# A graph kernel's prologue: order of the small groups' power, three fused weight products moved behind the first convolutions, fusion softmax between them

## The chip, the cores and the metric

One core of one Trainium2 chip. The metric is device time of one execution in microseconds; lower is better. The engines are PE (TensorE: matrix products and transpositions), DVE (VectorE), ACT (ScalarE), POOL (GpSimd) and SP (SyncE, which here only issues transfers).

## What is computed

Inputs are x (64 graphs of 128 nodes with 128 features) and adj (64 matrices of 128 x 128). Two blocks follow one another, each added to its input and layer-normalised:

```
x = layernorm(x + groups(x, adj))        # 5 groups of the first 25 nodes, two convolutions each
x = layernorm(x + gnn(x, adj != 0))      # 5 layers of message passing with a GRU cell
groups: A = adj_g + I; norm = dinv * A * dinv, dinv = (row sum of A) ** -0.5
        h = relu(norm @ (x_g @ W1[g]) + b1[g]); out_g = relu(norm @ (h @ W2[g]) + b2[g])
        sum over g of softmax(fusion_w)[g] * out_g, added into the nodes of the group
gnn, layer l: m = h @ weight[l]; agg = A.T @ m; gi = agg @ w_ih.T + b_ih; gh = h @ w_hh.T + b_hh
        r, z = sigmoid(i + h parts); n = tanh(i_n + r * h_n); h = (1 - z) * n + z * h
```

The kernel multiplies each layer's weight into the input weights beforehand (weight[l] @ w_ih.T, 128 x 384): these five products are the fused weights. For precision every operand of the large products is kept as a rounded high part and the remainder, its low part; a product is three matmuls.

## The kernel before, in words

The batch is cut into 4 chunks of 16 graphs, a chunk into 4 visits of 4 graphs. The message passing runs in 80 windows (5 layers x 4 visits x 4 chunks): window k makes the 18 gate products of one layer of one visit on PE, with the gates on ACT, DVE and POOL; the group convolutions of the next chunk are laid between the products of the current one by window number (the class Plan: adjacency, neighbours Y, hidden HA and HB, second SA and SB, outputs). Those of chunk 0 have no windows to lie between and make up the prologue, with the preparation of the weights. The order of work on each engine is written out by hand, one program per engine, and semaphores join them; an engine runs its program strictly in that order.

The prologue up to the first window (lines of the kernel before):

- Transfers. SP issues the small groups' adjacency rows, x rows (xt) and W2, then waits for ac_zero = 2, which POOL gives when it has cleared the later chunks' buffer (L450), and goes on with chunk 1's rows and the full x and adj of chunk 0. ACT issues w_ih, weight, w_hh, W1 and the bias rows (L586 to L590, between the high weights). POOL issues some adjacency and x rows, later eight adjacency rows of chunk 1 and the node mask (L452, L453).
- Degrees and power. DVE sums the rows (degrees, L705), POOL raises the sums to the power -1/2 in two instructions (power, L370: the large group's 4 tiles TA first, the small groups' 5 tiles TB second). DVE scales (scaled_part, L738) and expands the large group into block diagonals (spread, L748); POOL expands the small groups (spread, L376).
- PE runs 20 dummy transpositions (stay_warm, L1128), turns the weights (L1143 to L1151), makes fused weights 0 to 3 (L998) into the PSUM banks 3, 4, 6, 7, then 6 dummies, the transpositions of the block diagonals (first_adjacency, L1017, with 8 more dummies after the first), the products with x (neighbours, L1054), the transposition of the bias rows (L1162), the hidden and second products (L1063, L1073, L1080), the outputs (L1110, L1118), the mask's transposition (L1175), fused weights 4, 8 dummies, and the transposition of the gathered sums (back_visit, L1137) as soon as DVE has gathered them.
- High and low weights. ACT rounds each fused product into wf (high_weights, L504), DVE subtracts that from the PSUM bank for the low part (low_weights, L838). ACT makes the high parts of layers 0 to 3 ahead of the adjacency, 4 behind the outputs. DVE makes the low parts one by one between its other work.
- Fusion softmax. DVE subtracts the maximum (L903), POOL takes the exponential (L455), DVE divides (L909 to L914, signal b_ok); ACT's outputs (L543, L552) need it. DVE does this behind its copies second_b1 and second_b2.
- Then DVE gathers (L795), adds to x (L802), takes statistics (L828, L832); POOL makes deviations (L429 to L434) behind the ones of one adjacency visit (L407); ACT, DVE and POOL normalise; PE turns the result (L1187) and the windows begin.

Semaphores that matter: pow_ok (power), prep_f (a fused product is in its bank), prep_hi and prep_lo (its high, low part is made), b_ok, s_ps and o_ps (second products, outputs), mask_in, gathered.

Of the kernel before, what the change touches and what calls it, by code (L numbers as in the profile page):

```python
# [14 lines left out]
GATES = 3 * D  # L15
# [78 lines left out]
def made(k):  # L94

    return SLOTS + 1 if k == SLOTS - 1 else SLOTS if k == SLOTS else k + 1
# [33 lines left out]
def build(nc, x, adj, nodemask, W1, b1, W2, b2, fusion_w, weight, w_ih, w_hh, b_ih, b_hh, out):  # L130
# [3 lines left out]
    with ctx:  # L134
# [66 lines left out]
        wlt = cg[:].rearrange("p o (l d) -> p (o l) d", d=D)[:, 0:LAYERS, :]  # L201
        wit = ng[:, 0, 0:GATES]

        st1, ag1 = sb("st1", [128, SLOTS, SB, 6]), sb("ag1", [128, SLOTS, SB, 2])
# [7 lines left out]

        WF_BANKS = (3, 4, 6, 7, 3)

# [9 lines left out]
        def b1c(g, c):  # L224
# [9 lines left out]
        ac_pool_in = [sem(f"ac{c}_pool_in") for c in range(2)]  # L234
        wit_ok, wlt_ok, table_ok, sub_ok, f0_ps, x0_ok, a0_ok = map(sem, (
            "wit_ok", "wlt_ok", "table_ok", "sub_ok", "f0_ps", "x0_ok", "a0_ok"))
        ident_ok, ac_zero, dve_c, pool_c, exp_ok = map(sem, ("ident_ok", "ac_zero", "dve_c", "pool_c", "exp_ok"))
# [120 lines left out]
        def _(pool):  # L358
# [11 lines left out]
            def power(c):  # L370

                pool.wait_ge(deg_ok, c + 1)
                for some in (slice(0, len(TA)), slice(len(TA), NT)) if c == 0 else (slice(0, NT),):
                    nc.gpsimd.tensor_tensor(dinv[:, c, some], safe[:, some], minus_half[:, some], ALU.pow).then_inc(pow_ok, 1)
# [114 lines left out]
        def _(act):  # L489
# [11 lines left out]
            def high_weights(l):  # L501

                act.wait_ge(prep_f, l + 1)
                nc.scalar.copy(wf[:, l, 0, :], P[WF_BANKS[l]][:, 0:GATES]).then_inc(prep_hi, 1)  # L504

            def adjacency(c):
# [27 lines left out]
            def second_a(c):  # L534

                act.wait_ge(s_ps, 3 * c + 1)
                nc.scalar.copy(s2[0:ROWS[0], 0:4, :],
                               banks(c)["s"][0][0:ROWS[0], :].rearrange("p (t d) -> p t d", t=4)).then_inc(sa_ok, 1)
# [8 lines left out]
            def output_b(c):  # L547

                act.wait_ge(o_ps, 2 * c + 2)
                for g in range(1, NG):  # L550
                    a, b = group_cols(g)
                    nc.scalar.activation(part[:, a:b], banks(c)["o"][1][:, a:b], ACT.Relu, bias=fb2[:, g:g + 1],  # L552
                                         scale=fw[:, g:g + 1]).then_inc(ob_ok, 1)
# [36 lines left out]
            load_rows(NG * HC + NG + 3, b_hh.rearrange("(c h) -> c h", h=128))  # L590
            high_weights(2)
            high_weights(3)
            adjacency(0)
# [10 lines left out]
            output_a(0)  # L604
            output_b(0)
            high_weights(4)
            nc.scalar.copy(maskc[:], P[3][:, GATES:GATES + B]).then_inc(prep_a, 1)
# [80 lines left out]
        def _(dve):  # L688
# [49 lines left out]
            def scaled_part(tiles):  # L738

                part_ = slice(tiles[0], tiles[-1] + 1)  # L740
                dve.wait_ge(pow_ok, 1 if tiles is TA else 2)
                dve.wait_ge(prep_c, 4)
                link(TT(dinv[:, 0, part_], dinv[:, 0, part_], zero[:, part_], ALU.mult))
                if tiles is TB:
                    TT(am[:, part_, :], am[:, part_, :], dinv[:, 0, part_].unsqueeze(2).to_broadcast(am[:, part_, :].shape),
                       ALU.mult).then_inc(am_ok, 1)
# [88 lines left out]
            def low_weights(l):  # L835

                dve.wait_ge(prep_hi, l + 1 if l < 4 else l + 2)
                TT(wf[:, l, 1, :], P[WF_BANKS[l]][:, 0:GATES], wf[:, l, 0, :], ALU.subtract).then_inc(prep_lo, 1)  # L838

# [47 lines left out]

            degrees(0)
            low_weights(0)
            scaled_part(TA)  # L890
            spread(0)
            spread(1)
            scaled_part(TB)
            spread(2)
            spread(3)
            low_weights(1)
            adjacency(0)
            neighbours(0)
            dve.wait_ge(prep_hi, 5)
            TT(wh[:, 1, :], P[1][:, 0:GATES], wh[:, 0, :], ALU.subtract).then_inc(prep_lo, 1)  # L900
# [3 lines left out]
            hidden_b0(0)  # L904
            low_weights(2)
            second_b1(0)
            second_b2(0)
            dve.wait_ge(exp_ok, 1)
# [5 lines left out]
            TT(fb2[:], biasc[:, NG * HC:BI], fw[:], ALU.mult).then_inc(b_ok, 1)  # L914
            low_weights(3)
            gather(0)
# [9 lines left out]
            dve.wait_ge(prep_a, 2)  # L926
            low_weights(4)
            lo_neighbours(0, PG)
# [5 lines left out]
            for w in ALL_WINDOWS:  # L934
# [46 lines left out]
                if w.sg + 2 < CHUNKS and w.i == Plan.SCALED:  # L981
                    scaled(w.sg + 2)
            final = B // SB - 1
            norm2(final - 3)
# [8 lines left out]
        def _(pe):  # L993
# [23 lines left out]
            def first_adjacency():  # L1017

                pe.wait_ge(bda_ok, 1)
                turn_adjacency(0, 0)  # L1020
                stay_warm(8, P[5])
                pe.wait_ge(bdb_ok, 1)
                turn_adjacency(0, 4)
                turn_adjacency(0, 5)
                pe.wait_ge(bda_ok, 2)
                turn_adjacency(0, 1)
                pe.wait_ge(bdb_ok, 2)
                turn_adjacency(0, 6)
                pe.wait_ge(bda_ok, 3)
                turn_adjacency(0, 2)  # L1030
                pe.wait_ge(bdb_ok, 3)
                turn_adjacency(0, 7)
                pe.wait_ge(bda_ok, 4)
                turn_adjacency(0, 3).then_inc(t_ps, 1)
                pe.wait_ge(bdb_ok, 4)
                turn_adjacency(0, 8).then_inc(t_ps, 1)
# [117 lines left out]
            pe.wait_ge(wlt_ok, 1)  # L1154
            for l in range(4):
                fused_weights(l)
            stay_warm(6, P[5])
            first_adjacency()
# [15 lines left out]
            pe.wait_ge(mask_in, 16)  # L1174
            TR(P[3][:, GATES:GATES + B], maskr[:], ident[0:B, 0:B])  # L1175
            fused_weights(4)
            stay_warm(8, P[4])
            pe.wait_ge(gathered, ADDS)
            for visit in range(SLOTS):
                back_visit(visit)  # L1180
            stay_warm(18, PR)
            for _ in range(12):
                MM(PR[:, 0:128], wh[:, 0, 0:128], wh[:, 0, 128:256], start=True, stop=True)

# [22 lines left out]
            def enter(visit, bank):  # L1207
# [6 lines left out]
                turn(bank, entering(visit)).then_inc(X_ps, 1)  # L1214

            enter(0, PL)
            pe.wait_ge(a0_ok, 1)
            aggregate(0, PG, entering(0))

            for w in ALL_WINDOWS:  # L1220
                k, s = w.k, w.slot
                xhi, xlo = hhi[:, s, :], hlo[:, s, :]
                pe.wait_ge(hi_ok, made(k))
                if k == 0:

                    pe.wait_ge(x0_ok, SLOTS)
                    gates = ((PR, 0), (PH, 2), (PZ, 1))
# [62 lines left out]
                if k == 0:  # L1290
                    pe.wait_ge(a0_ok, 2)
                    pe.wait_ge(prep_lo, 6)
                    aggregate(1, PT, entering(1))
# [43 lines left out]
```

## Time and profile before

| | |
|---|---|
| time, median of 3 runs | 546.04 us (545.37 to 546.91) |
| profiled execution, span from first to last instruction | 544.4 us; the page gives it no time of its own |
| PE busy | 519.5 us, 95% of the span |
| DVE / ACT / POOL busy | 437.8 / 368.6 / 250.2 us |
| mean granted TensorE clock | 0.983 of full |

The span is the time from the first to the last instruction; a run's time also holds what lies around it. Shares are averages over the prologue (about 36 us before PE turns the first normalised visit), the windows and a short end.

### The profile page before, as it was taken

Reading aid. Unit: us, or ns where it says so; the run is one execution under the profiler, and the core shown is the slowest. Engines: PE = TensorE matmul, PEld = TensorE weight load, DVE = VectorE, ACT = ScalarE, POOL = GpSimd, SP = SyncE. Lnnn points to the kernel's source line nnn. Section 1 sums busy time; section 2 is a strip of 40 time slices with the busy share of each in tenths; the row PEclk is TensorE's granted clock in tenths of the full one; section 3 lists DMA queues with packets and bytes.
Section 4 is the critical chain, followed back from the end, with each engine's and each line's share of the span. In section 5 each row is a group of like instructions: output and inputs, shape, how many; then the busy total and the mean of one; then the engine's idle time right before and its main releaser. Section 6 shows DMA issues by size and latency. Waiting matters only on the chain.

```text
span 544.4 us, 8517 instructions
## 1 busy us (share of the span) xinstructions
PE 519.5 (95%) x2991; PEld 443.9 (82%) x2991; DVE 437.8 (80%) x965; ACT 368.6 (68%) x681; POOL 250.2 (46%) x301
## 2 busy tenths in 40 slices
PE   7998899999999999999999999999999999999970
PEld 5886788888888889888888888888888888888850
DVE  4488566689989986789988986778988998878785
ACT  2446566577786676787776676687795678777644
POOL 6659222258642254448652245446542244423235
PEclk8999899999999999999999999999999999999995
DMA  5867610000000010000000000000000000100002
GB/s 141 198 178 183 161 32 5 1 0 1 2 0 1 1 32 20 21 20 21 0 2 1 0 1 21 20 20 20 0 2 1 1 1 20 39 20 0 1 0 78
DMA packets 35564, 17.29 MB, mean 32 GB/s; under 512 B 4306, under 2 KB 35483, under 8 KB 35523
## 3 DMA queue, kind: packets, MB, share of 16 engines
q1 hardware_dynamic: 32489, 15.12, 10.5%
q10 hardware_dynamic: 2393, 1.41, 0.9%
q8 instruction: 24, 0.39, 0.3%
q0 software_dynamic: 640, 0.22, 0.3%
q14 instruction: 18, 0.14, 0.1%
HBM read 12.54 MB, written 4.19 MB: 31 GB/s over the span
## 4 chain that ended last, share of the span: by engine, by line
PE 88%; DVE 6%; ACT 2%; DMA 1%; issue 1%; ACTq 1%; POOL 1%; DVEq 0%; POOLq 0%
PE p L1200 19%; PE p L1202 19%; PE p L1201 19%; PE p L1194 13%; PE p L1187 8%; PE p L1080 3%; PE p L1054 2%; PE p L1073 1%; PE p L1063 1%; DVE hT L866 1%; PE p L998 1%; DMA zg<-in_L_gnn_weight_dram 1%; DVE cg L965 1%; PE p L1004 1%; DVE cg L968 1%
## 5 line engine op out<-in xcount | busy, mean ns | idle before, releaser
L470 POOL TENSOR_TENSOR dg<-hT,ng 128x512 f32<-128x512 f32 x80 | 125.9, 1574 | 266.2 <-ACT ng L672 266.2
L1200 PE MATMUL p<-ghi,wf 128*128 128x512 f32 x240 | 101.2, 422 | 2.0 <-DVE glo L858 1.9
L1200 PE MATMUL p<-hhi,wh 128*128 128x512 f32 x237 | 100.1, 422 | 0.0
L1202 PE MATMUL p<-ghi,wf 128*128 128x512 f32 x240 | 94.5, 394 | 0.0
L1201 PE MATMUL p<-glo,wf 128*128 128x512 f32 x240 | 93.6, 390 | 0.0
L1202 PE MATMUL p<-hhi,wh 128*128 128x512 f32 x237 | 93.3, 394 | 0.0
L1201 PE MATMUL p<-hlo,wh 128*128 128x512 f32 x237 | 92.6, 391 | 0.0
L965 DVE SCALAR_TENSOR_TENSOR cg<-p,biasc,rg 128x512 f32<-128x512 f32 x80 | 59.8, 748 | 39.0 <-ACT rg L656 38.0
L656 ACT ACTIVATE rg<-p,gb 128x512 f32<-128x512 f32 x80 | 55.4, 692 | 36.6 <-PE p L1202 30.9
L672 ACT ACTIVATE ng<-cg,biasc 128x512 f32<-128x512 f32 x80 | 57.9, 724 | 23.1 <-DVE cg L968 22.9
L1194 PEld LDWEIGHTS p<-an,nat 128*128 128x128 f32 x512 | 67.2, 192 | 7.4 <-DVE glo L858 2.2
L1194 PE MATMUL p<-an,nat 128*128 128x128 f32 x512 | 67.9, 276 | 2.0 <-DVE glo L858 2.0
L852 DVE TENSOR_TENSOR hlo<-hT,hhi 128x512 fp32r<-128x512 f32 x76 | 66.7, 878 | 1.0
L670 ACT ACTIVATE zg<-p,gb 128x512 f32<-128x512 f32 x80 | 55.0, 688 | 17.8 <-PE p L1202 17.8
L968 DVE TENSOR_TENSOR cg<-cg,p 128x512 f32<-128x512 f32 x80 | 55.0, 687 | 8.7 <-DVE cg L965 0.5
L858 DVE TENSOR_TENSOR glo<-p,ghi 128x512 fp32r<-128x512 f32 x80 | 55.2, 690 | 7.3 <-ACT ghi L623 7.2
L866 DVE TENSOR_TENSOR hT<-ng,dg 128x512 f32<-128x512 f32 x80 | 56.9, 712 | 2.8
L1187 PE MATMUL p<-ident,hT 128*128 128x128 f32 x320 | 49.0, 276 | 7.4 <-DVE hT L866 7.3
L864 DVE TENSOR_TENSOR dg<-zg,dg 128x512 f32<-128x512 f32 x80 | 55.2, 690 | 0.0
L1187 PEld LDWEIGHTS p<-ident,hT 128*128 128x128 f32 x320 | 38.6, 142 | 18.8 <-DVE hT L866 12.0
L1202 PEld LDWEIGHTS p<-ghi,wf 128*128 128x128 f32 x240 | 45.0, 188 | 10.5
L652 ACT COPY nat<-p 128x512 f32<-128x512 f32 x64 | 37.6, 588 | 22.7 <-PE p L1187 21.8
(147 smaller groups left out, 855.2 us busy)
## 6 DMA issues: line engine op xcount, KB each, us to landing
xn<-in_x_dram SPq DMA_DIRECT2D x8, 512.0 KB, 4.8
an<-in_adj_dram SPq DMA_DIRECT2D x8, 512.0 KB, 7.2
out_dram<-xn SPq DMA_DIRECT2D x16, 256.0 KB, 2.3
xt<-in_x_dram SPq DMA_DIRECT2D x16, 50.0 KB
w<-in_L_gnn_W_dram ACTq DMA_DIRECT2D x1, 640.0 KB, 6.1
w<-in_L_gnn_W_dram SPq DMA_DIRECT2D x1, 640.0 KB, 6.3
zg<-in_L_gnn_weight_dram ACTq DMA_DIRECT2D x1, 320.0 KB, 4.0
xt<-in_x_dram SPq DMA_DIRECT2D x8, 36.0 KB
```

The source lines that it names most:

```text
L470: nc.gpsimd.tensor_tensor(dg[:, w.k % 2, :], hT[:, w.slot, :], ng[:, w.k % 2, :], ALU.subtract).then_inc(d_ok, 1)
L656: nc.scalar.activation(rg[:, p, :], PR[:], ACT.Sigmoid, bias=gb[:, 0:1]).then_inc(r_ok, 1)
L672: nc.scalar.activation(ng[:, p, :], cg[:, p, :], ACT.Tanh, bias=bin_).then_inc(n_ok, 1)
L852: TT(hlo[:, m % SLOTS, :], hT[:, m % SLOTS, :] if source is None else source[:], hhi[:, m % SLOTS, :], ALU.subtract).then_inc(lo_ok, 1)
L866: TT(hT[:, s, :], ng[:, p, :], dg[:, p, :], ALU.add).then_inc(h_ok, 1)
L965: STT(cg[:, p, :], PH[:], bhn, rg[:, p, :], ALU.add, ALU.mult).then_inc(t1_ok, 1)
L968: TT(cg[:, p, :], cg[:, p, :], PI[:], ALU.add).then_inc(c_ok, 1)
L1187: last = TR(bank[:, q * 128:(q + 1) * 128], src(q), ident[:])
L1194: last = MM(bank[:, q * N:(q + 1) * N], src(q), an[:, b + q, :], start=True, stop=True)
L1200: MM(bank[:], w[:, 0, cols], xhi, start=start, stop=False)
L1201: MM(bank[:], w[:, 0, cols], xlo, start=False, stop=False)
L1202: return MM(bank[:], w[:, 1, cols], xhi, start=False, stop=stop)
```

## The change

- POOL raises the small groups to the power first; DVE scales them first and then scales and expands the large group. The low weights of layers 0 and 1 come behind these.
- PE makes only fused weights 0 and 1 ahead of the adjacency; 2, 3 and 4 come behind the outputs, layer 3 into bank 0 instead of 7. The dummies after the fused weights (6), inside first_adjacency (8) and behind fused weights 4 (8) are left out; the later dummies write another bank.
- ACT copies fused products 2 to 4 also into SBUF (kept, a view of s2, which is free then); DVE subtracts from there, in windows 3, 4 and 5. PE waits for kept_ok ahead of the first turn and the first window, and for the low parts at the first window of layers 2 to 4; ACT's next write of s2 waits for the last subtraction.
- DVE does the softmax ahead of second_b1 and second_b2.

```diff
@@ -200,6 +200,7 @@
         wl = zg[:].rearrange("p o (l d) -> p (o l) d", d=D)[:, 0:LAYERS, :]
         wlt = cg[:].rearrange("p o (l d) -> p (o l) d", d=D)[:, 0:LAYERS, :]
         wit = ng[:, 0, 0:GATES]
+        kept = s2[:].rearrange("p (l q) d -> p l (q d)", l=3)
 
         st1, ag1 = sb("st1", [128, SLOTS, SB, 6]), sb("ag1", [128, SLOTS, SB, 2])
         rs1, nm1 = sb("rs1", [128, SLOTS, SB]), sb("nm1", [128, SLOTS, SB])
@@ -210,7 +211,7 @@
         PR, PH, PZ, PI, PT, PG, PL, PM = P
 
 
-        WF_BANKS = (3, 4, 6, 7, 3)
+        WF_BANKS = (3, 4, 6, 0, 3)
 
         ALONE = dict(adj=(P[0], P[2]), y=(P[5], P[4]), ha=(P[0], P[2]), hb=(P[5], P[3]), s=(P[4], P[1], P[0]),
                      o=(P[2], P[5]))
@@ -232,8 +233,8 @@
         ac_in = [sem(f"ac{c}_in") for c in range(CHUNKS)]
         ac_act_in = sem("ac_act_in")
         ac_pool_in = [sem(f"ac{c}_pool_in") for c in range(2)]
-        wit_ok, wlt_ok, table_ok, sub_ok, f0_ps, x0_ok, a0_ok = map(sem, (
-            "wit_ok", "wlt_ok", "table_ok", "sub_ok", "f0_ps", "x0_ok", "a0_ok"))
+        wit_ok, wlt_ok, table_ok, sub_ok, f0_ps, x0_ok, a0_ok, kept_ok = map(sem, (
+            "wit_ok", "wlt_ok", "table_ok", "sub_ok", "f0_ps", "x0_ok", "a0_ok", "kept_ok"))
         ident_ok, ac_zero, dve_c, pool_c, exp_ok = map(sem, ("ident_ok", "ac_zero", "dve_c", "pool_c", "exp_ok"))
         prep_t, prep_a, prep_f, prep_hi, prep_lo, fw_ok, b_ok = map(sem, (
             "prep_t", "prep_a", "prep_f", "prep_hi", "prep_lo", "fw_ok", "b_ok"))
@@ -370,7 +371,7 @@
             def power(c):
 
                 pool.wait_ge(deg_ok, c + 1)
-                for some in (slice(0, len(TA)), slice(len(TA), NT)) if c == 0 else (slice(0, NT),):
+                for some in (slice(len(TA), NT), slice(0, len(TA))) if c == 0 else (slice(0, NT),):
                     nc.gpsimd.tensor_tensor(dinv[:, c, some], safe[:, some], minus_half[:, some], ALU.pow).then_inc(pow_ok, 1)
 
             def spread(c):
@@ -502,6 +503,8 @@
 
                 act.wait_ge(prep_f, l + 1)
                 nc.scalar.copy(wf[:, l, 0, :], P[WF_BANKS[l]][:, 0:GATES]).then_inc(prep_hi, 1)
+                if l >= 2:
+                    nc.scalar.copy(kept[:, l - 2, :], P[WF_BANKS[l]][:, 0:GATES]).then_inc(kept_ok, 1)
 
             def adjacency(c):
 
@@ -534,6 +537,8 @@
             def second_a(c):
 
                 act.wait_ge(s_ps, 3 * c + 1)
+                if c == 1:
+                    act.wait_ge(prep_lo, 6)
                 nc.scalar.copy(s2[0:ROWS[0], 0:4, :],
                                banks(c)["s"][0][0:ROWS[0], :].rearrange("p (t d) -> p t d", t=4)).then_inc(sa_ok, 1)
 
@@ -588,8 +593,6 @@
             high_weights(1)
             load_rows(NG * HC + NG, b_ih.rearrange("(c h) -> c h", h=128))
             load_rows(NG * HC + NG + 3, b_hh.rearrange("(c h) -> c h", h=128))
-            high_weights(2)
-            high_weights(3)
             adjacency(0)
             neighbours(0)
             act.wait_ge(prep_t, 4)
@@ -603,6 +606,8 @@
             act.wait_ge(b_ok, 1)
             output_a(0)
             output_b(0)
+            high_weights(2)
+            high_weights(3)
             high_weights(4)
             nc.scalar.copy(maskc[:], P[3][:, GATES:GATES + B]).then_inc(prep_a, 1)
 
@@ -738,7 +743,7 @@
             def scaled_part(tiles):
 
                 part_ = slice(tiles[0], tiles[-1] + 1)
-                dve.wait_ge(pow_ok, 1 if tiles is TA else 2)
+                dve.wait_ge(pow_ok, 1 if tiles is TB else 2)
                 dve.wait_ge(prep_c, 4)
                 link(TT(dinv[:, 0, part_], dinv[:, 0, part_], zero[:, part_], ALU.mult))
                 if tiles is TB:
@@ -834,8 +839,14 @@
 
             def low_weights(l):
 
-                dve.wait_ge(prep_hi, l + 1 if l < 4 else l + 2)
-                TT(wf[:, l, 1, :], P[WF_BANKS[l]][:, 0:GATES], wf[:, l, 0, :], ALU.subtract).then_inc(prep_lo, 1)
+                if l < 2:
+                    dve.wait_ge(prep_hi, l + 1)
+                    product = P[WF_BANKS[l]][:, 0:GATES]
+                else:
+                    dve.wait_ge(prep_hi, l + 2)
+                    dve.wait_ge(kept_ok, l - 1)
+                    product = kept[:, l - 2, :]
+                TT(wf[:, l, 1, :], product, wf[:, l, 0, :], ALU.subtract).then_inc(prep_lo, 1)
 
             def half_norm1(visit, some):
 
@@ -886,25 +897,20 @@
                 last.then_inc(ln2_st, 1)
 
             degrees(0)
+            scaled_part(TB)
+            scaled_part(TA)
+            for t in TA:
+                spread(t)
             low_weights(0)
-            scaled_part(TA)
-            spread(0)
-            spread(1)
-            scaled_part(TB)
-            spread(2)
-            spread(3)
             low_weights(1)
             adjacency(0)
             neighbours(0)
-            dve.wait_ge(prep_hi, 5)
+            dve.wait_ge(prep_hi, 3)
             TT(wh[:, 1, :], P[1][:, 0:GATES], wh[:, 0, :], ALU.subtract).then_inc(prep_lo, 1)
             dve.wait_ge(fw_in, 16)
             link(nc.vector.tensor_reduce(fmx[:], fw[:], AX.X, ALU.max, negate=True))
             TS(fw[:], fw[:], fmx[:], None, ALU.add).then_inc(sub_ok, 1)
             hidden_b0(0)
-            low_weights(2)
-            second_b1(0)
-            second_b2(0)
             dve.wait_ge(exp_ok, 1)
             link(nc.vector.reduce_sum(fsum[:], fw[:], AX.X))
             link(nc.vector.reciprocal(fsum[:], fsum[:]))
@@ -912,7 +918,8 @@
             dve.wait_ge(prep_a, 1)
             TT(gb[:], biasc[:, BI:BI + 2], biasc[:, BI + 3:BI + 5], ALU.add)
             TT(fb2[:], biasc[:, NG * HC:BI], fw[:], ALU.mult).then_inc(b_ok, 1)
-            low_weights(3)
+            second_b1(0)
+            second_b2(0)
             gather(0)
             ones(0)
             add_visit(0)
@@ -924,7 +931,6 @@
             add_visit(3)
             lo_state(0, PL)
             dve.wait_ge(prep_a, 2)
-            low_weights(4)
             lo_neighbours(0, PG)
             norm1(2)
             ones(1)
@@ -980,6 +986,8 @@
                     lo_neighbours(k + 2, PG)
                 if w.sg + 2 < CHUNKS and w.i == Plan.SCALED:
                     scaled(w.sg + 2)
+                if k in (3, 4, 5):
+                    low_weights(k - 1)
             final = B // SB - 1
             norm2(final - 3)
             leave(final - 1, PT)
@@ -1018,7 +1026,6 @@
 
                 pe.wait_ge(bda_ok, 1)
                 turn_adjacency(0, 0)
-                stay_warm(8, P[5])
                 pe.wait_ge(bdb_ok, 1)
                 turn_adjacency(0, 4)
                 turn_adjacency(0, 5)
@@ -1152,9 +1159,8 @@
             last.then_inc(prep_t, 1)
             pe.wait_ge(wit_ok, 1)
             pe.wait_ge(wlt_ok, 1)
-            for l in range(4):
-                fused_weights(l)
-            stay_warm(6, P[5])
+            fused_weights(0)
+            fused_weights(1)
             first_adjacency()
             neighbours(0)
             nr = NG * HC + NG + 6
@@ -1173,14 +1179,15 @@
             output_b(0)
             pe.wait_ge(mask_in, 16)
             TR(P[3][:, GATES:GATES + B], maskr[:], ident[0:B, 0:B])
+            fused_weights(2)
+            fused_weights(3)
             fused_weights(4)
-            stay_warm(8, P[4])
             pe.wait_ge(gathered, ADDS)
             for visit in range(SLOTS):
                 back_visit(visit)
-            stay_warm(18, PR)
+            stay_warm(18, PG)
             for _ in range(12):
-                MM(PR[:, 0:128], wh[:, 0, 0:128], wh[:, 0, 128:256], start=True, stop=True)
+                MM(PG[:, 0:128], wh[:, 0, 0:128], wh[:, 0, 128:256], start=True, stop=True)
 
             def turn(bank, src):
                 for q in range(SB):
@@ -1213,6 +1220,7 @@
                     pe.wait_ge(ln1_dve, 1)
                 turn(bank, entering(visit)).then_inc(X_ps, 1)
 
+            pe.wait_ge(kept_ok, 1)
             enter(0, PL)
             pe.wait_ge(a0_ok, 1)
             aggregate(0, PG, entering(0))
@@ -1221,8 +1229,11 @@
                 k, s = w.k, w.slot
                 xhi, xlo = hhi[:, s, :], hlo[:, s, :]
                 pe.wait_ge(hi_ok, made(k))
+                if w.i % SLOTS == 0 and 2 <= w.l and w.sg == 0:
+                    pe.wait_ge(prep_lo, w.l + 2)
                 if k == 0:
 
+                    pe.wait_ge(kept_ok, 3)
                     pe.wait_ge(x0_ok, SLOTS)
                     gates = ((PR, 0), (PH, 2), (PZ, 1))
                     for bank, g in gates:
@@ -1289,7 +1300,6 @@
                 product(PZ, wl_now, 1, xhi, xlo, False, True).then_inc(z_ps, 1)
                 if k == 0:
                     pe.wait_ge(a0_ok, 2)
-                    pe.wait_ge(prep_lo, 6)
                     aggregate(1, PT, entering(1))
                 if k in (1, 2):
                     pe.wait_ge(glo_ok, 2 * k - 1)
```

## Rows read from the trace of the kernel before

**Rows 1.** The profile page: span, chain by engine, and one group of its costliest (columns named there).
```profile
span 544.4 us, 8517 instructions
...
PE 88%; DVE 6%; ACT 2%; DMA 1%; issue 1%; ACTq 1%; POOL 1%; DVEq 0%; POOLq 0%
...
L852 DVE TENSOR_TENSOR hlo<-hT,hhi 128x512 fp32r<-128x512 f32 x76 | 66.7, 878 | 1.0
```

**Rows 2.** Chain of waits, 8 to 60 us: start, us, what.
```profile
9.73 4.51 PE p L998 x8
14.24 0.66 PE p L1131 x6
...
15.86 0.59 PE p L1004 x7
...
16.97 2.22 PE p L1054 x18
```

**Rows 3.** Stretches: PE, PEld, DVE, ACT, POOL busy (x); PEclk, DMA share, GB/s.
```profile
5.00:10.00 5.00, 3.40 (x18) 2.65 (x18) 1.43 (x5) 2.62 (x5) 3.23 (x8) 1.00 0.65 163
10.00:15.00 5.00, 5.00 (x17) 2.94 (x16) 2.83 (x9) 1.92 (x4) 3.66 (x8) 0.66 0.89 260
...
55.00:60.00 5.00, 3.56 (x21) 2.77 (x19) 4.30 (x8) 4.36 (x8) 0.53 (x1) 1.00 0.22 58
60.00:70.00 10.00, 9.36 (x55) 8.60 (x56) 3.68 (x9) 3.73 (x9) 3.00 (x2) 0.83 0.77 192
```

**Rows 4.** PE in order of time: start, us, instruction.
```profile
28.82 0.91 PE L998 MATMUL p<-ng,cg 128*128 128x384 f32 x2
```

**Rows 5.** POOL in order of time; idle before and its releaser in brackets.
```profile
9.82 2.19 POOL L374 TENSOR_TENSOR dinv<-safe,minus_half 128x4 f32<-128x4 f32 x2 [1.48 <-DVE safe L727]
13.36 1.56 POOL L395 TENSOR_TENSOR bdb<-am,ksel 72x144 f32<-72x144 f32 x5 [1.34 <-DVE am L745]
...
16.27 4.73 POOL L263 DMA_DIRECT2D ac<-in_adj_dram  x8 [0.29 <-POOL fused L451]
...
21.52 1.26 POOL L455 TENSOR_TENSOR fw<-euler,fw 128x5 f32<-128x5 f32 x1
29.74 2.02 POOL L407 TENSOR_SCALAR an<-an 128x512 f32<-128x512 f32 x1 [6.96 <-DMA an<-in_adj_dram]
33.79 0.20 POOL L429 TENSOR_SCALAR rs<-ag 128x4 f32<-128x4 f32 x1 [2.02 <-DVE ag L832]
```

**Rows 6.** VectorE in order of time, prologue.
```profile
13.19 0.90 DVE L751 SCALAR_TENSOR_TENSOR bda<-am,dinv,ksel 100x100 f32<-100x100 f32 x2
...
16.56 1.18 DVE L760 TENSOR_SCALAR nb<-p,dinv 72x72 f32<-72x72 f32 x5 [2.00 <-PE p L1004]
...
25.35 0.42 DVE L779 COPY s<-p 72x256 f32<-72x256 f32 x1 [2.02 <-PE p L1080]
...
27.20 0.14 DVE L909 TENSOR_REDUCE fsum<-fw 128x1 f32<-128x5 f32 x1
...
28.00 0.55 DVE L838 TENSOR_TENSOR wf<-p,wf 128x384 fp32r<-128x384 f32 x1
```

**Rows 7.** Stretches of half a microsecond, PE alone: busy (x), PEclk, DMA share, GB/s.
```profile
14.50:15.00 0.50, 0.50 (x7) 1.00 1.18 314
...
16.50:17.00 0.50, 0.06 (x2) 1.00 0.07 22
```

**Rows 8.** DMA issues, 0 to 50 us: KB, median us from issue to landing.
```profile
maskr<-in_nodemask_dram POOLq DMA_DIRECT2D x1, 32.0 KB, 6.7
```

**Rows 9.** ScalarE in order of time, prologue.
```profile
30.07 0.49 ACT L504 CAST wf<-p 128x384 fp32r<-128x384 f32 x1
...
35.58 0.88 ACT L562 ACTIVATE xn<-xn,nm,rs 128x128 f32<-128x128 f32 x2 [4.91 <-POOL nm L434]
```

**Rows 10.** VectorE in order of time, behind windows 3 and 4.
```profile
76.93 0.75 DVE L965 SCALAR_TENSOR_TENSOR cg<-p,biasc,rg 128x512 f32<-128x512 f32 x1 [2.25 <-ACT rg L656]
...
81.46 1.06 DVE L773 TENSOR_SCALAR hb<-p,biasc 128x144 f32<-128x144 f32 x4 [1.03 <-PE p L1073]
```

## The prediction

> **What bounds the kernel now.** I read the page first, then the chain of waits, then the engines in order of time over the first 45 us, because everything the change moves lies there or has its price there. The chain that ended last runs through PE for 88% of the span [rows 1]: from about 61 us to the end PE is hardly ever without work, so nothing done on the other engines in the 80 windows shows unless PE waits for it, and a microsecond taken out of the prologue is a microsecond taken from the end. The prologue's own chain [rows 2] is PE as well: eight records of fused weights (four layers) from 9.73 to 14.24, then dummy transpositions (14 of them, with one real one among them) to 15.86, 0.59 us of real ones, and from 16.97 the convolutions. The clock explains why the fused weights are so long: between 10 and 15 us the mean granted clock was 0.66, which is 3.4 us at 0.5 (1.2 GHz) and the rest at 1 (2.4 GHz), after five microseconds in which PE had work for 3.40 [rows 3]; the one layer made later took 0.91 us with its tail [rows 4], not 4.51 / 4 = 1.13.
>
> **What the change does, step by step** (times are those of the profiled execution).
>
> **1. Power and expansion.** The two powers take 2.19 us on POOL from 9.82, and POOL then idles 1.34 us, since the small groups, which POOL itself expands, come second [rows 5]. With the small groups first their power is ready at about 10.95 (half of 2.19), VectorE scales them while POOL makes the second power, and POOL's five expansions (1.56 us) start at about 12.05 instead of 13.36: done at 13.6, not 14.9. VectorE's four expansions can start at about 12.25; the pair beside POOL's work took 0.90 [rows 6], so four take at most 1.8, to 14.0. The two low-weight subtractions now come behind them, 0.55 each [rows 6], to 15.1.
>
> **2. PE to the end of the adjacency.** Two of four layers go (half of 4.51, 2.25 us) and with them the dummies from 14.24 to 15.86, 1.62 us: 3.9 us less work ahead of the 0.59 us of transpositions. Not all of it is gained: PE is free at 12.0 but the last expansion comes at about 14.0, so the adjacency ends at about 14.3 instead of 16.45, 2.15 earlier.
>
> **3. Neighbours.** These are 18 records, 2.22 us [rows 2]. The large group's 8 follow at once (14.8 to 15.8). The small groups need VectorE's five scalings, 1.18 us [rows 6], which now start at 15.1, behind the second subtraction, and end at 16.3. PE's 10 records trail them: about 16.9, instead of 19.18, 2.3 earlier.
>
> **4. A wait that comes up behind it.** PE next transposes the bias rows, before directly behind the neighbours at 19.19 [rows 2]; their four loads and those of the small groups' x were issued by 13.0, and no view shows when they landed. Bounds: not before the queues drained, not after 19.19. The DMA share was 1.18 at 14.5 to 15.0 and 0.07 at 16.5 to 17.0 [rows 7], so I take 17.2, nearest to the second row, and the step becomes 1.95 instead of 2.3. Were they as early as 15, the gain stays 2.3; as late as 19, there is none.
>
> **5. The convolutions** shift as one piece, if the clock holds, since PE works there without a gap. The softmax is moved into a place where VectorE waited 2.02 us for PE (before 25.35) and takes 0.80 (27.20 to 28.00) [rows 6]. Its exponential is POOL's, 1.26 us, behind eight adjacency loads that POOL issues from 16.27 on and the mask's [rows 5]; all of that moves up by 1.3, so it ends at 21.5, the softmax at 22.4, and the copy behind it is wanted at 25.35 - 1.95 = 23.4. Cover left: 1.0 us. If POOL is later than that, second_b1 and all PE work behind it wait.
>
> **6. Fused weights 2 to 4 after the outputs.** Before, one layer and eight dummies lay in PE from 28.82 until the gathered sums came at 30.98, 2.16 us [rows 2, 4]. Three layers take 2.0 to 2.25 (0.65 to 0.75 each: the second record overlaps the first one's tail) and at most 3 x 0.91 = 2.7: zero to 0.55 us late; I take zero. The mask that PE waits for ahead of them took 6.7 us to land [rows 8] from its issue right behind those loads, at 16.27 + 4.73 = 21.0, so it was there at 27.7 and was read before 28.82; issued 1.3 earlier it is there at 26.4, wanted at about 26.7. ScalarE's six copies and the mask's (7 x 0.49 at most, 3.4 us, of which 1.0 was there before) go into its wait of 4.91 us before 35.58 [rows 9]: nothing, with 2.5 left.
>
> **7. POOL ahead of the layer norm.** It waits for the adjacency until 29.74, makes ones of it for 2.02, to 31.76, and is wanted at 33.79 [rows 5], after the change at 31.84. The load is released by POOL's memset, 1.3 us earlier; even unmoved it would just do. Nothing.
>
> **8. Low weights in windows 3, 4 and 5.** VectorE then waits for others for 2.25, 1.03 and, the third time, longer than that [rows 10]; two of the three waits stand there. A subtraction costs between 0.55 and, by the mean of a wider one whose inputs both lie in SBUF, 0.88 [rows 6, 1]: covered. The Trainium skill (SBUF — State Buffer, "Who interferes with whom") says that a DVE instruction with two SBUF inputs contends with a GpSimd instruction that reads SBUF, which would speak for the upper end, as that mean does; the sum is zero by either. The removed subtraction between the first state and neighbours stood in a wait for ScalarE: nothing.
>
> **Sum:** 2.15 by step 2, 2.3 by step 3, cut to 1.95 by step 4; nothing from 5 to 8. The span goes from 544.4 [rows 1] to 542.45. The page gives no time of its own for this execution; the median of the runs, 546.04, is 1.6 above its span, and I carry that over: **544.1 us**. About 0.3% (1.6 us) is what a measurement of this kernel can tell from no change, so the forecast lies only just on the faster side.
>
> **The rivals.**
> **A. The clock takes the gain.** The 22 dummies kept PE busy; without them it waits between 12.0 and 14.8 for most of the time. Before, five microseconds with work for 3.56 were followed by ten with a mean clock of 0.83, again 3.4 us at 0.5 [rows 3]. If such a stretch falls on the neighbours and first hidden products, it loses 1.7 of 1.95: 545.8. For it: PE's work from 12.7 to 14.3 is sparse. Against: the stretch between 10 and 15 ended while PE was fed without a break, and the neighbours and the convolutions are dense. The Trainium skill (TensorE: Matmul & The Clock Gate, "What's actually happening") puts it as a rule: the throttled state is the default and activity releases it; that speaks against taking the dummies out, and the rows agree that idle time precedes the fall.
> **B. Slower.** The same mechanism, lasting: half clock from about 14.8 until well into the second convolution, two such stretches. The convolutions are bound by PE, so 6.8 us at 0.5 cost 3.4, more than the 1.95: 547.5. It turns to the slower side once PE runs 3.9 us of this work at half clock. Against: rows 3 show two such stretches, 50 us apart, and none that lasts.
> **C. More gain.** The loads are there at 16.9 (2.3 gained, 543.7), or the half clock after 60 us [rows 3] does not come when the same work arrives 2 us earlier; it costs up to 1.7, so 544.1 - 1.7 = 542.4.
> **D. The wait only moves.** The bias rows land near 19, or POOL's longer way to the exponential holds the softmax: PE waits where it worked before, 546.0.
>
> **The numbers.** Forecast 0.52, A 0.16, B 0.08, C 0.16, D 0.08. About three quarters of the forecast's own spread (half a microsecond each way, from steps 4 and 6) lies past 0.3%: 0.39, with C 0.55 for faster. The rest of it, A and D make 0.37 within 0.3%, B 0.08 slower. The range runs from C's lower value to a little past D: 542.3 to 546.3, and leaves out B and the tail of C.
>
> **What would show it.** Right: the first expansions on POOL at about 12.1; PE's adjacency ending near 14.3; a short PE idle before the bias rows, which start near 17.2; the gathered sums transposed near 29.0; ScalarE's wait before the first norm shrunk to under 2 us; first window's products 1.9 us earlier, and window 20 as well. Wrong: half clock after 14 us (A, B), a PE wait before the bias rows beyond 18 or a VectorE wait for the exponential (D), a second copy in VectorE held up in windows 3 to 5, or a late mask in front of the fused weights.

## The result, and the profile after

| | before | changed |
|---|---|---|
| median | 545.35 us (10 executions, 543.45 to 546.95) | 548.04 us (10 executions, 546.27 to 549.13) |
| ratio to before, 95% interval | 1 | 1.0045 [1.0026, 1.0064] |
| span of the profiled execution | 544.4 us | 546.7 us |

The changed kernel is 0.45% slower by the ratio (the medians lie 2.7 us apart), where 1.95 us less was forecast. In the experiments further down, one execution of the filled kernel (754 us) and one of the reordered kernel (2974 us) were disturbed and are left out of the ratios; the second was the profiled one, so no trace of that kernel is read. (Line numbers in the rows of the changed kernel and of the experiments are those of each kernel; the operands name the step. L1006 is now a fused product, L1061 the neighbours, L1070 and L1080 the hidden products, L1087 the second ones.)

The chain of waits of the changed kernel, to be held against [rows 2]:

```profile
10.63 5.81 DMA xt<-in_x_dram
16.44 0.04 issue
16.49 2.45 PE p L1061 x10
18.93 0.22 PE p L1168
19.16 2.96 PE p L1070 x4
...
30.54 2.13 PE p L1006 x6
32.67 0.45 PE p L1144 x4
```

PE in order of time in the same execution (the bracket is PE's idle time before the row and what ended it):

```profile
12.95 0.29 PE L1012 MATMUL p<-ident,bda 100*100 100x100 f32 x1 [1.87 <-DVE bda L756]
...
14.66 1.11 PE L1061 MATMUL p<-na,xt 100*128 100x100 f32 x8 [0.44 <-ACT na L515]
16.49 2.45 PE L1061 MATMUL p<-nb,xt 72*128 72x72 f32 x10 [0.72 <-DMA xt<-in_x_dram]
...
19.09 3.03 PE L1070 MATMUL p<-ya,w 128*128 128x400 f32 x4
21.91 2.41 PE L1080 MATMUL p<-yb,w 128*128 128x144 f32 x16
...
32.51 1.69 PE L1144 MATMUL p<-ident,fused 128*25 128x128 f32 x14
```

The same records of small groups, hidden products and back transposition in the kernel before:

```profile
17.91 1.28 PE L1054 MATMUL p<-nb,xt 72*128 72x72 f32 x10
...
19.28 1.61 PE L1063 MATMUL p<-ya,w 128*128 128x400 f32 x4
20.73 1.96 PE L1073 MATMUL p<-yb,w 128*128 128x144 f32 x16
...
30.98 1.93 PE L1137 MATMUL p<-ident,fused 128*25 128x128 f32 x16 [0.37 <-DVE fused L795]
```

And stretches of the changed kernel, with the columns of [rows 3]:

```profile
10.00:15.00 5.00, 2.69 (x16) 1.49 (x15) 3.50 (x11) 1.79 (x6) 4.71 (x10) 1.00 0.89 263
15.00:20.00 5.00, 4.28 (x20) 3.56 (x20) 1.65 (x6) 1.27 (x4) 5.00 (x9) 0.60 0.55 115
20.00:25.00 5.00, 5.00 (x28) 4.01 (x27) 2.12 (x10) 1.82 (x5) 1.27 (x2) 0.72 1.13 277
...
50.00:60.00 10.00, 10.00 (x48) 8.38 (x48) 5.77 (x9) 6.49 (x13) 5.49 (x11) 0.83 0.41 102
60.00:70.00 10.00, 7.68 (x47) 6.88 (x46) 4.51 (x11) 4.32 (x10) 3.53 (x2) 0.83 0.62 143
```

The first neighbours start at 14.66, 2.31 us earlier than before [rows 2]: up to there the change does what it was meant to. But between 10 and 15 us PE has work for only 2.69 of 5, against 5.00 before [rows 3]: it waits 1.87 us for the first block diagonal, 0.44 for the scaled adjacency and, just behind, 0.72 for the x rows. Then the granted clock is 0.60 and 0.72 in the next two stretches: 4.0 and 2.8 us at 0.5, 6.8 us in all (from about 16.0 to 22.8). The three groups of products it falls on take 2.45, 3.03 and 2.41 us, against 1.28, 1.61 and 1.96 before. With the wait for the x rows, that turns 2.31 us of lead into 1.53 of lag: the back transposition starts at 32.51 instead of 30.98. The remaining 0.8 of the 2.3 us between the spans comes later: this execution has half clock twice in windows 1 to 3 (mean 0.83 between 50 and 60 and again between 60 and 70), that of before once. The profile is one execution, but the mean granted clock is on record for all: 0.968 to 0.976 in the ten of the changed kernel, 0.977 to 0.989 in the 35 of the kernel before that were timed beside the first four experiments.

### The profile page after: what moved, and what is told of

Its sections match the earlier page's. It is cut to its first block, busy times and chain, and to the rows that moved or that the text cites. A ratio compares the mean times of both kernels' runs of the same rounds, so it can differ in the third digit from the quotient of the medians.

```text
span 546.7 us, 8482 instructions
## 1 busy us (share of the span) xinstructions
PE 520.0 (95%) x2969; PEld 443.9 (81%) x2969; DVE 436.8 (80%) x965; ACT 369.3 (68%) x684; POOL 250.1 (46%) x301
## 4 chain that ended last, share of the span: by engine, by line
PE 89%; DVE 5%; SPq 2%; ACT 1%; DMA 1%; issue 1%; POOL 1%; ACTq 0%; POOLq 0%; DVEq 0%
PE p L1207 20%; PE p L1209 20%; PE p L1208 19%; PE p L1201 13%; PE p L1194 8%; PE p L1087 3%; PE p L1061 2%; PE p L1080 1%; PE p L1070 1%; DMA xt<-in_x_dram 1%; SPq L269 1%; PE p L1125 1%; SPq L264 1%; PE p L1117 1%; DVE st L892 1%
## 5 line engine op out<-in xcount | busy, mean ns | idle before, releaser
L877 DVE TENSOR_TENSOR hT<-ng,dg 128x512 f32<-128x512 f32 x80 | 55.4, 692 | 2.8
```

What stands on the lines that cost most here:

```text
L877: TT(hT[:, s, :], ng[:, p, :], dg[:, p, :], ALU.add).then_inc(h_ok, 1)
```

## The experiments

Each was timed together with the kernel before on the same chip; ratios are to that kernel. Its median there was 545.41 us beside the first four, 545.67 beside the next four and 544.96 beside the last two.

### Two parts of the change alone, on the kernel before

The 22 dummies taken out (behind the fused weights, inside the adjacency, behind fused weights 4), nothing moved:

```diff
-            stay_warm(6, P[5])
...
-                stay_warm(8, P[5])
...
-            stay_warm(8, P[4])
```

> The kernel before without its 22 dummies and nothing else. Theory: the four layers of fused weights keep PE at work until about 14.2, so the clock is back before the neighbours and stays; the adjacency ends about 1 us earlier, 544.3 to 545.3. Rival (the dummies alone hold the clock, whatever real work stands there): half clock in the convolutions as in the changed kernel, 547 or more.

Measured: 545.61 us, ratio 0.9998 [0.9977, 1.0019]. PE in order of time:

```profile
10.06 4.08 PE L998 MATMUL p<-ng,cg 128*128 128x384 f32 x8
13.98 0.25 PE L1004 MATMUL p<-ident,bda 100*100 100x100 f32 x1
...
28.51 0.27 PE L1173 MATMUL p<-ident,maskr 64*128 64x64 f32 x1 [0.79 <-DMA maskr<-in_nodemask_dram]
28.71 0.91 PE L998 MATMUL p<-ng,cg 128*128 128x384 f32 x2
29.70 3.53 PE L1136 MATMUL p<-ident,fused 128*25 128x128 f32 x16
```

With four layers of fused weights in front, the clock was 1.00 from 15 to 25 us in this execution, over the neighbours and the first convolution, so the rival falls. The gain hoped for is not there either, and the median lies 0.3 us above the band: the first neighbours start 0.97 us earlier (16.00 for 16.97), but PE then waits 0.79 us for the mask, and the back transposition takes 3.53 us for 1.93, at half clock, behind the place where the other eight dummies had stood.

The order of powers, expansions and softmax, nothing else:

```diff
-                for some in (slice(0, len(TA)), slice(len(TA), NT)) if c == 0 else (slice(0, NT),):
+                for some in (slice(len(TA), NT), slice(0, len(TA))) if c == 0 else (slice(0, NT),):
...
+            scaled_part(TB)
+            scaled_part(TA)
+            for t in TA:
+                spread(t)
             low_weights(0)
...
             low_weights(1)
...
```

> The kernel before with the order of the powers, scalings and expansions and the place of the softmax from the changed kernel; fused weights and dummies as before. Theory: PE's fused weights at half clock still set the adjacency's end, so the time is that of the kernel before within 0.7 us, 544.6 to 546.0. Rival (the new order on VectorE or POOL is what costs): slower by 1.5 us or more.

Measured: 546.50 us, ratio 1.0011 [0.9992, 1.0030]: no change that can be told, half a microsecond outside the band, and short of the rival's 1.5. So neither part alone makes the loss: taking the dummies out costs nothing that can be told while the four fused weights stand there, and neither does the order. The third part, three fused weights moved while all dummies stay and the order is the old one, was not tried alone.

### The dummies put back into the changed kernel

```diff
             fused_weights(1)
+            stay_warm(6, P[5])
             first_adjacency()
...
                 turn_adjacency(0, 0)
+                stay_warm(8, P[5])
```

> The changed kernel with the 14 dummy transpositions ahead of the neighbours put back where they stood (6 behind the fused weights, 8 behind the first block diagonal). Theory (half clock from 16.0 to 22.8 us in the changed kernel costs about 3 us, because PE has too little work between 11 and 16.5 us): the clock does not fall there, or for one stretch instead of two, and the time drops by 1.5 to 3 us against the changed kernel's 548.0, to 545 to 546.5. Rival (the loss comes from the late x rows and the moved fused weights themselves): within 0.5 us of 548.0, since dummies add no useful work.

Measured: 545.02 us, ratio 0.9995 [0.9975, 1.0015]; the loss is gone with 14 instructions that compute nothing. The clock, which was still at half over most of the fused weights, is back before the neighbours and stays:

```profile
10.00:15.00 5.00, 5.00 (x28) 3.54 (x26) 3.22 (x9) 0.96 (x2) 4.71 (x10) 0.72 0.92 259
15.00:20.00 5.00, 4.56 (x31) 3.81 (x31) 2.83 (x9) 3.22 (x9) 5.00 (x9) 1.00 0.57 128
20.00:25.00 5.00, 5.00 (x47) 5.00 (x47) 2.25 (x10) 1.74 (x6) 1.36 (x2) 1.00 1.19 278
```

Dummies sized to the three waits:

```diff
             fused_weights(1)
+            stay_warm(14, P[7])
             first_adjacency()
+            stay_warm(4, P[7])
...
                     if c == 0 and half is TB:
+                        stay_warm(5, P[7])
                         pe.wait_ge(xt_in, 16 * n_runs(XT_SP))
```

> The changed kernel with 23 dummies sized to PE's waits: 14 behind the fused weights, 4 between adjacency and neighbours, 5 ahead of the wait for the small groups' x rows. Theory: full clock from 13 to 40 us, bias rows transposed at about 17.5, back transposition at about 29.2, 3.3 us earlier than in the changed kernel: 544.0 to 545.0, about 1 us faster than before. Rival (the moved work itself costs): 547 or more.

Measured: 543.51 us, ratio 0.9975 [0.9957, 0.9993]. PE in order of time, and two stretches:

```profile
10.96 1.69 PE L1139 MATMUL p<-ident 128*128 128x128 f32 x14
12.95 0.29 PE L1012 MATMUL p<-ident,bda 100*100 100x100 f32 x1 [0.30 <-DVE bda L756]
...
16.15 1.35 PE L1062 MATMUL p<-nb,xt 72*128 72x72 f32 x10
17.43 0.23 PE L1171 MATMUL p<-ident,rows 21*128 21x21 f32 x1
17.60 1.61 PE L1071 MATMUL p<-ya,w 128*128 128x400 f32 x4
19.04 1.96 PE L1081 MATMUL p<-yb,w 128*128 128x144 f32 x16
...
27.24 2.20 PE L1006 MATMUL p<-ng,cg 128*128 128x384 f32 x6
29.28 1.91 PE L1145 MATMUL p<-ident,fused 128*25 128x128 f32 x16
```

```profile
15.00:20.00 5.00, 5.00 (x36) 4.22 (x36) 2.29 (x8) 2.46 (x6) 5.00 (x9) 1.00 0.52 125
20.00:25.00 5.00, 5.00 (x48) 5.00 (x47) 2.29 (x11) 1.67 (x5) 1.30 (x2) 1.00 1.22 274
```

The clock stays at 1.00, the first transposition starts at the same 12.95, and the three groups of products take 1.35, 1.61 and 1.96 us: 2.97 less than in the changed kernel. That is the price of the half clock in this place. The back transposition starts at 29.28, 3.23 us earlier than in the changed kernel. The time lies half a microsecond below its band of 544.0 to 545.0, and by the ratio beats the kernel before; no execution that counts has a mean clock under 0.982.

### Which wait lets the clock fall

The same dummies divided: the first 14 alone, and the other 9 alone.

> The changed kernel with only the first 14 of the 23 dummies of the filled one: those behind the fused weights, in PE's wait for the first block diagonal. Theory that the longest wait (1.9 us before 12.95) lets the clock fall: as the filled kernel within 0.7 us, 543.5 to 545. Theory that the three waits do it together: between the two, 545 to 547, with half clock in the neighbours or hidden products. Rival that the later waits alone do it: 547.5 or more.

> The changed kernel with only the other 9 dummies: 4 behind the adjacency and 5 ahead of the wait for the small groups' x rows. Theory that the longest wait lets the clock fall: 547 to 548.5, half clock still between 14 and 23 us. Three waits together: 545 to 547. Rival that the later waits do it: 543.5 to 545.

Measured: 546.41 us, ratio 1.0001 [0.9981, 1.0021], and 545.38 us, ratio 1.0001 [0.9974, 1.0028]. Both lie between the filled kernel (0.9975) and the changed one (1.0045), as the theory of three waits together has it, but the intervals overlap with that of the filled kernel, and the second with that of the changed one too: that neither set alone does all is likely, not shown. With the nine alone the clock still fell, earlier and for a shorter time (stretches of that kernel):

```profile
10.00:15.00 5.00, 3.43 (x19) 2.36 (x18) 3.72 (x12) 1.99 (x6) 4.70 (x10) 0.88 0.93 263
15.00:20.00 5.00, 5.00 (x28) 4.42 (x28) 1.84 (x6) 1.33 (x5) 4.87 (x9) 0.78 0.62 142
20.00:25.00 5.00, 5.00 (x46) 4.87 (x45) 2.23 (x12) 2.59 (x7) 1.19 (x1) 1.00 1.18 274
```

That is 1.2 + 2.2 = 3.4 us at half clock instead of 6.8. With the 14 alone the one profiled execution kept 1.00 until 55 us, against the half clock in the neighbours that the theory asked for, and had no wait for the x rows. But it was one of the two fastest of twelve (544.34 us, mean clock 0.985); most of the others were longer, by up to 3 us, with mean clocks of 0.976 to 0.983, and where their clock fell is not known. Its PE:

```profile
15.77 1.28 PE L1061 MATMUL p<-nb,xt 72*128 72x72 f32 x10
...
28.89 1.91 PE L1144 MATMUL p<-ident,fused 128*25 128x128 f32 x16
```

### The half clock in windows 1 to 3

```diff
+                if k == 1:
+                    pe.wait_ge(hT_ok, 2)
+                    stay_warm(14, PM)
                 pe.wait_ge(ghi_ok, k + 1)
...
                 if w.feed and k >= 2:
+                    if k == 2:
+                        stay_warm(14, PM)
                     pe.wait_ge(glo_ok, k + 2)
```

On the filled kernel, and on the kernel before:

> The filled kernel and 14 dummies each in PE's two waits for VectorE in windows 1 and 2 (2.0 and 2.3 us). Theory: the half clock at about 47 to 54 and 60 to 67 us, which costs up to 1.7 us a time and comes in some executions, goes away: median 542.5 to 543.5, all executions within 1.5 us of the lowest, faster than both kernels. Rival (the dummies hold up PE, or those stretches cost nothing): 543.5 or more, as the filled kernel.

> The kernel before with the 14 dummies in each of the two waits of windows 1 and 2, prologue untouched. Theory: the stretch of half clock after 60 us goes, worth up to 1.7 us where it came: 543.7 to 544.8. Rival: 545.4, unchanged.

Measured: 543.56 us, ratio 0.9956 [0.9938, 0.9975], executions from 543.01 to 545.10; and 545.07 us, ratio 0.9980 [0.9960, 1.0001]. The first is 2.4 us below its kernel before by the ratio, but its median is just outside its band and no better than the 543.51 of the filled kernel, and its executions spread by 2.1 us where 1.5 was expected; so its rival, that the later stretches cost nothing there, is not refuted. The second lies outside its band by 0.3 us and cannot quite be told from no change. The second one's trace matters most, because its execution, the fastest of its twelve, had full clock over the fused weights too. The kernel before, windows filled, PE in order of time:

```profile
9.58 2.82 PE L998 MATMUL p<-ng,cg 128*128 128x384 f32 x8 [0.38 <-ACT cg L583]
...
15.12 1.11 PE L1054 MATMUL p<-na,xt 100*128 100x100 f32 x8 [0.44 <-ACT na L512]
16.07 1.34 PE L1054 MATMUL p<-nb,xt 72*128 72x72 f32 x10
17.33 0.23 PE L1162 MATMUL p<-ident,rows 21*128 21x21 f32 x1
...
28.91 1.93 PE L1137 MATMUL p<-ident,fused 128*25 128x128 f32 x16
```

Four layers of fused weights take 2.82 us here, not 4.51 [rows 2], and the back transposition starts at 28.91. The changed kernel with its waits filled starts it at 29.28, and with the 14 alone, where the x rows came in time, at 28.89. So at equal clock these traces leave nothing to gain from moving the fused weights.

### The clock alone, against the clock and the moved work

Eight more dummies ahead of the fused weights, meant to have the clock up when they start, on both of these:

```diff
+            stay_warm(5, PM)
             pe.wait_ge(wl_in, 16)
...
+            stay_warm(3, PM)
             pe.wait_ge(wit_ok, 1)
```

> The kernel before with dummies in its waits only: 5 ahead of the wait for the layer weights, 3 ahead of the first fused weights, 14 in each of the waits of windows 1 and 2. No work is moved. Theory (the clock is all there was to gain: at full clock the kernel before reaches the back transposition at 28.9 us, the changed one with dummies at 29.2): full clock over the fused weights in most executions, median 543.0 to 544.0, as good as the changed kernel with all waits filled. Rival (the moved fused weights have a gain of their own of 1 us or more): 544.5 or more, behind it.

> The changed kernel with 23 dummies in the prologue and 14 in each of windows 1 and 2, and the same 8 early dummies as its partner. Theory: 543.0 to 543.8, within 0.5 us of the partner. Rival (moved work has a gain of its own): 1 us or more faster than the partner.

Measured: 543.16 us (542.89 to 543.97), ratio 0.9965 [0.9947, 0.9984], and 543.35 us (542.99 to 544.23), ratio 0.9976 [0.9961, 0.9991]. The kernel before with dummies in its waits, no work moved, cannot be told from the changed one with its waits filled; both beat the kernel before and the changed one, and the executions of each agree within 1.3 us, where the kernel before beside them spread from 542.96 to 548.86. Two stretches of the first:

```profile
10.00:15.00 5.00, 4.83 (x31) 3.52 (x29) 2.96 (x10) 2.08 (x5) 4.15 (x9) 1.00 0.94 273
...
50.00:60.00 10.00, 8.75 (x59) 7.34 (x58) 7.86 (x10) 6.36 (x13) 4.62 (x5) 1.00 0.45 112
```

The fastest executions of the kernel before, 542.96, were there already; the dummies make nearly all of them like that.

## Why the prediction was wrong

The time moved the other way than forecast; rival B, given 0.08, has the mechanism and nearly the time (547.5 forecast, 548.0 measured). Its 6.8 us at half clock are the size measured, though they lie from 16.0 to 22.8, in the neighbours and the first convolution, and not from 14.8 into the second. Step by step:

- **Step 1, power and expansion: right.** POOL's expansions started at 11.87 (12.05 forecast), the first block diagonal was there at 12.95.
- **Step 2, adjacency near 14.3: right.** The neighbours of the large group started at 14.66. But with what this step counted as "3.9 us less work" gone, the clock fell, and with 14 dummies back in its place it did not; the step treated PE's freed time as neutral.
- **Step 3, neighbours done at 16.9: wrong twice.** VectorE's scalings were done at 15.81 (16.3 forecast), but the small groups' x rows landed at 16.44 by the chain, so PE waited 0.72 us; and the ten records then took 2.45 us, at half clock, to 18.93.
- **Step 4, a load behind: right in kind.** It was the x rows and not the bias rows on which PE waited. With the clock held, the bias rows were transposed at 17.43, 0.2 from the 17.2 taken.
- **Step 5 is the step that failed: "the convolutions shift as one piece, if the clock holds".** It did not hold. From 16.0 to 22.8 us it was 0.5 (1.2 GHz), which cost 2.97 us in the three groups of products, against the filled kernel. The size was in rival B already (6.8 us at half clock, 3.4 us); the chance given to it was too small. The argument against B was that rows 3 "show two such stretches, 50 us apart, and none that lasts". One execution of a kernel that had dummies in these waits could not show what the clock does without them. The other claim of this step, that the softmax fits in, was right: with the clock held it ended at 22.22 (22.4 forecast), and VectorE still waited 1.45 us for PE behind it.
- **The sum's base.** The 1.95 us were counted against an execution in which the fused weights ran at half clock. With full clock there the kernel before starts the back transposition at 28.91, the changed one with dummies at 28.89 to 29.46 in four profiles, so the gain is there only where the clock is low. The clock of 0.66 between 10 and 15 us was a state of that execution (0.72 in the same place with the dummies out, 1.00 with dummies in later windows only) and not a property of the work, which one profile could not tell.
- **Step 6:** the three layers take 2.04 us to the back transposition, in the filled kernel, where the sums were gathered at 28.93 and PE came at 29.28, 0.35 late: inside the bound of 0 to 0.55, not at the zero that was taken. In the changed kernel ScalarE still waits 2.88 us before the norm: nothing, as step 6 has it with 2.5 left, though the forecast's list of signs says under 2.
- **Step 7: right.** POOL was done with the ones at 29.9 in the changed kernel and waited 5.37 us.
- **Step 8: covered, though dearer than its bound.** Rows of the changed kernel (VectorE in order of time):

```profile
75.72 1.00 DVE L849 TENSOR_TENSOR wf<-s,wf 128x384 fp32r<-128x384 f32 x1
...
82.52 1.02 DVE L849 TENSOR_TENSOR wf<-s,wf 128x384 fp32r<-128x384 f32 x1
```

A subtraction from SBUF took 1.00 to 1.02 us, against 0.54 from PSUM for layers 0 and 1 in the same execution and 0.88 as the forecast's upper bound. Each began beside a POOL subtraction that reads SBUF (74.69 to 76.31, 81.48 to 83.12, 89.49 to 91.12). The Trainium skill (SBUF — State Buffer, "Who interferes with whom") says that a DVE instruction with two SBUF inputs contends with a GpSimd instruction that reads SBUF. The traces agree: VectorE's wider subtraction hlo from hT and hhi, 128x512, both in SBUF, took 0.68 us at 76.65 with POOL idle, and 1.00 us at 73.69 in the kernel before, where POOL subtracted from 72.52 to 74.14. That this is the cause was not tried by itself. No PE wait followed.

The Trainium skill's rule on the clock (TensorE: Matmul & The Clock Gate, "What's actually happening": the throttled state is the default and activity releases it) was quoted as speaking against the change. The runs agree: with less work on PE the clock fell, with 14 or 23 dummies put back it held, and where four fused weights stood in front it held over the first convolution without dummies. So here it was not the dummies as such that counted but whether PE had something to do.

## What to carry to other kernels

An instruction that computes nothing may be what a stage's clock rests on: before removing filler or moving real work out of a stage bound by PE, look at what stays in that stage, and put back about as much as the new waits are long. A gain counted from one profile holds for the clock of that execution; where executions spread further than the gain (3.5 us here, for a gain of 1.95), price the step at both levels. And when the clock is the term, try the filler alone first: here it gave 0.35% without moving any work, and 0.24% with the work moved, with intervals that overlap.

## What was not expected of the hardware

The clock fell although PE's longest wait in front of it was 1.87 us, with transpositions and the first neighbours between the waits. It does not seem to be tied to one wait: the longest filled alone, and the shorter two filled alone, gave ratios of 1.0001 each, against 1.0045 with none and 0.9975 with all, though the intervals overlap. And the same program at the same place has half clock in one execution and not in another: the fused weights took 4.51 us for eight records in the profile of the kernel before, 2.82 us in that of the same kernel with dummies only in later windows.
